# Remainders of chunk 6's sums on VectorE, a semaphore of their own for turned sums, six mask copies ahead of an addition

## The chip, the core and the metric

The kernel runs on one core of a Trainium2 chip. The metric is the device time of one execution in microseconds (us), the median of several runs. PE is TensorE, DVE is VectorE, ACT is ScalarE, POOL is GpSimd, and SP is the engine whose queue issues the DMAs here.

## The reference

Two residual layers over x of shape (2, 1024, 512), in float32:

```python
x = x + gated_delta(layernorm(x), Wq, Wk, Wv, Wo, Wb, bb, Wd, bd)
x = x + ffn(layernorm(x), w1, w2, w3)

# gated_delta: q, k, beta, delta of 64, v of 128; one state S (64 x 128) per batch
S = beta[t][:, None] * S + delta[t][:, None] * outer(k[t], v[t])
o[t] = q[t] @ S                      # then @ Wo

# ffn: weights reduced to -1, 0, 1: clip(round(w / mean|w|))
hidden = sigmoid(x @ Q(w1).T) * (x @ Q(w2).T)     # 512 -> 1408
y = hidden @ Q(w3).T                              # 1408 -> 512
```

## The kernel before

**Tiling.** The 1024 steps are cut into eight chunks (0 to 7) of 128 steps, with both batches side by side. Chunks go through the attention layer one by one. For the second layer two chunks make a group, so there are four groups (g = 0 to 3) of 512 tokens. Group g runs eleven hidden tiles (units u = 0 to 10 of 128 hidden columns), and then four down tiles (m = 0 to 3, one for each chunk and batch), each a sum of 22 matmuls of 512 columns (`down`, L1604). While PE works on group g, the other engines take chunks 2g+2 and 2g+3 through attention, the second normalisation and the split into two 16-bit parts, so that group g+1 can start.

**Fast groups.** Groups 2 and 3 (`FAST`) use a Strassen-like scheme with seven products instead of eight (`product1` to `product7`, each four matmuls of 256 columns, L1622). Products 1, 2 and 4 read the tokens themselves, turned into `xT_N`. Products 3, 5, 6 and 7 read sums and differences of tokens (`xsum`), turned into `xT_S`. Unit u's order on PE is 1, then 5 and 4 of the unit before, 6, 2, then 3 of the unit before, and 7. `product1(g, 0)` is pulled into the last down tile of the group before: it is issued ahead of that tile's last four matmuls. Its result is copied by ACT (`seed`, L936), and `product6(g, 0)`, which follows the down tile, waits for that copy (`seeded`). `product3(g, u)` accumulates into the bank that DVE's `up_b(g, u)` (L1354) must have read.

**Preparing a chunk for a fast group.** DVE `apply` (L1218) writes the normalised tokens, after POOL's six small operations of `norm2` (L523 to L529) have given the scale. The sums are made by DVE (`sums`, L1164 to L1167) for chunks 5 and 7, and by POOL (`sums0`, `sums1`) for chunks 4 and 6. ACT rounds tokens (`xhiN`, L823) and sums (`xhiS`, L828) to 16 bits. The remainders, value minus rounded value, are made by DVE for tokens (`xlo`, L1223). For the sums they are made by DVE for chunks 5 and 7 (`xloS`, one instruction, L1170), and by POOL for chunks 4 and 6 (`xlo`, four instructions, L607). SP then issues two DMA transposes for the chunk (`turn_x`): L434 for tokens, L437 for sums. Both add 16 to `xT_in`, and PE waits once, ahead of `product1(g + 1, 0)`, for the full count of both chunks of the group:

```python
if m == DT - 1 and n == 2 * HT - 4:
    pe.wait_ge(xT_in, 64 * g + 128)
    product1(g + 1, 0)
down(g, m, n, PARTS_IN_TURN)
```

`apply` of chunk 7 waits for `xlo0_ready` of chunk 6, that is for the remainders of chunk 6's sums.

**Order.** Every engine's order is written by hand. Tables such as `DVE_FAST` give for a step the place for chunk 2g+2 and for chunk 2g+3. A negative place u stands for place 15 + u of the group before. `DOWN` (22) is the place in front of the first addition of a fast group (`add_out(g, 0)`, L1309). Steps of one place run in the order of the table. A step at place 14 of a group that isn't fast stands in front of that group's last addition, `add_out(1, 3)`.

**Masks.** For each chunk seven predicated copies (`masks`, L1181) and an eighth (L1189) bring the attention scores of the levels from PSUM into `sc`; PE's `o` step (L1476 to L1485) waits for the eighth. For chunk 6 all stand at place 0 of group 2: behind `add_out(1, 3)`, ahead of `up_b(2, 0)`.

Of the kernel before, what the change touches and what calls it, by code (L numbers as in the profile page):

```python
# [16 lines left out]
def build_gated_delta_ternary_ffn(nc, x, Wq, Wk, Wv, Wo, Wb, bb, Wd, bd, w1, w2, w3, out):  # L17
# [31 lines left out]
    with ctx:  # L49
# [64 lines left out]
        class Scratch:  # L114
            def __init__(self, flat):
# [60 lines left out]
        xhi_ready, xlo0_ready, xlo1_ready, xT_in = (sem("xhi_ready"), sem("xlo0_ready"), sem("xlo1_ready"),  # L176
                                                    sem("xT_in"))
# [77 lines left out]
        def sums_at(which):  # L255
# [21 lines left out]
                    "chainE": (None, 4.5), "masks0": (0, 6.5), "masks1": (0, 7), "masks2": (0, 7.5),  # L277
                    "masks3": (0, 8), "state": (2, None), "resid0": (5, 10.5), "resid1": (5.5, 11),
                    "xlo": (DOWN, DOWN + 1), "xloS": (None, DOWN + 1), "norm2a": (8.5, 11.5), "norm2b": (9, HT + 1),
                    "apply": (10, DOWN), "sums": (None, DOWN)}  # L280
        ACT_FAST = {"gt": (0, None), "oT": (2, 9), "xhiN": (HT, HT + 2), "xhiS": (HT + 1, HT + 2)}
        POOL_FAST = {"fetch": (-1, 0), "sums0": (10, None), "sums1": (11, None), "norm2": (9, HT + 1),
                     "xlo": (HT + 1, None)}
# [65 lines left out]
        def is_fast(c):  # L349

            return c // 2 in FAST

# [40 lines left out]
        def _(sp_):  # L393
# [35 lines left out]
            def turn_x(c):  # L429

                if is_fast(c):
# [6 lines left out]
                                            flat_S[c % 2]).then_inc(xT_in, 16)  # L438
# [53 lines left out]
        def _(pool):  # L492
# [108 lines left out]
            def xlo(c):  # L601
                if c > 1:
                    pool.wait_ge(xT_in, 16 * B * (c - 1))
                if is_fast(c):
                    pool.wait_ge(xhi_ready, B * c + 2)
# [98 lines left out]
        def _(act):  # L704
# [105 lines left out]
            def attn(s, c):  # L810
# [9 lines left out]
                if s == "xhiN":  # L820
                    act.wait_ge(xT_in, 16 * B * (c - 1))
# [4 lines left out]
                if s == "xhiS":  # L826
                    act.wait_ge(sums_ready, c - 2 * FAST[0] + 1)
                    nc.scalar.activation(split_S[c % 2][:, :, 0, :], xsum[:, :, :], ACT.Copy).then_inc(xhi_ready, 1)  # L828
                if s == "xhi":
                    if c > 1:  # L830
                        act.wait_ge(xT_in, 16 * B * (c - 1))
# [177 lines left out]
        def _(dve):  # L1009
# [119 lines left out]
            def attn(s, c):  # L1129
# [31 lines left out]
                if s == "sums":  # L1161
                    dve.wait_ge(xn2_ready, B * c + 2)
                    dve.wait_ge(xhi_ready, B * c)
                    nc.vector.tensor_tensor(xsum[:, 2, :], A11(0), A11(1), ALU.subtract)  # L1164
# [46 lines left out]
                if s == "apply":  # L1211
                    dve.wait_ge(rstd2_ready, c + 1)
                    if c > 0:
                        dve.wait_ge(xhi_ready, B * c)
                        dve.wait_ge(xlo0_ready, c)
# [4 lines left out]
                if s == "xlo" and is_fast(c):  # L1220
                    dve.wait_ge(xT_in, 16 * B * (c - 1))
# [4 lines left out]
                elif s == "xlo":  # L1226
                    if c > 1:
                        dve.wait_ge(xT_in, 16 * B * (c - 1))
# [171 lines left out]
        def _(pe):  # L1400
# [161 lines left out]
            def group(g):  # L1562
                pe.wait_ge(xT_in, 64 * g + 64)
                for u in range(UNITS):
# [15 lines left out]
                    else:  # L1580
                        m = u - HT
                        bank_free(g, 2 * HT + m)
                        for n in range(2 * HT):
# [4 lines left out]
                            if m == DT - 1 and n == 2 * HT - 4 and g + 1 in FAST:  # L1588
                                pe.wait_ge(xT_in, 64 * g + 128)
# [48 lines left out]
            def product6(g, u):  # L1638

                pe.wait_ge(seeded, fast_n(g, u) + 1)  # L1640
# [104 lines left out]
```

## Time and profile before

| | |
|---|---|
| Median of three runs | 322.31 us (322.20 to 322.46) |
| The profiled execution | 321.82 us |
| Its span, first to last instruction | 320.1 us |
| PE, busy | 311.6 us (97%), 2416 matmuls |
| DVE, busy | 226.9 us (71%) |
| ACT, busy | 170.4 us (53%) |
| POOL, busy | 150.0 us (47%) |
| Granted TensorE clock, mean | 0.999 of full speed |

The span is the time on which the steps of one execution can be placed; 1.7 us of the execution's own time lie outside it. Start times below are us from the start of the span. A matmul's end is modelled, so the steps between starts say more on PE than the busy time. A bracket at the end of a timeline row is the idle time of the engine before it and what ended that.

### The profile page before, as it was taken

How to read it: one execution, taken by the hardware profiler on the slowest of the kernel's cores; microseconds unless marked ns; L12 is line 12 of the kernel's file. 1: busy time of each engine (PE TensorE's matmuls, PEld its weight loads, DVE VectorE, ACT ScalarE, POOL GpSimd, SP SyncE). 2: the span in 40 equal slices, each digit the busy share in tenths (PEclk: the TensorE clock that was granted, in tenths of full speed). 3: DMA queues.
4: the chain of work that ended last, by engine and by line, in shares of the span. 5: the costliest groups of instructions: out<-in, count | busy, mean ns of one | idle time of the engine just before them, and what ended most of it. 6: DMA issues, size and time to landing. Idle time of an engine off the chain costs nothing.

```text
span 320.1 us, 6755 instructions
## 1 busy us (share of the span) xinstructions
PE 311.6 (97%) x2416; PEld 200.9 (63%) x2416; DVE 226.9 (71%) x510; ACT 170.4 (53%) x369; POOL 150.0 (47%) x395
## 2 busy tenths in 40 slices
PE   7999999999999999999999999999999999999996
PEld 5888779874545444445445445678976448888545
DVE  6889889899998866277898898559676543454401
ACT  3587896879863772323325215347655216777300
POOL 7298215589932105992016832634468501544300
PEclk9999999999999999999999999999999999999999
DMA  6999900475852441500000807000000691000011
GB/s 177 380 386 394 393 16 0 64 136 104 129 101 49 81 86 45 121 33 2 0 2 0 116 36 180 36 2 0 2 3 0 69 252 45 2 0 2 0 68 66
DMA packets 51953, 28.62 MB, mean 89 GB/s; under 512 B 43728, under 2 KB 44496, under 8 KB 51920
## 3 DMA queue, kind: packets, MB, share of 16 engines
q1 hardware_dynamic: 51600, 28.19, 34.5%
q8 instruction: 19, 0.31, 0.4%
q14 instruction: 14, 0.11, 0.1%
q10 hardware_dynamic: 320, 0.00, 0.0%
HBM read 13.89 MB, written 4.19 MB: 57 GB/s over the span
## 4 chain that ended last, share of the span: by engine, by line
PE 70%; DVE 12%; DMA 5%; issue 4%; SPq 3%; POOL 3%; ACT 3%; DVEq 0%; POOLq 0%; ACTq 0%
PE ffn L1575 17%; PE ffn L1604 15%; PE ffn L1622 14%; PE pd L1622 5%; PE lev L1496 4%; PE ffn L1420 3%; DMA x_sb<-in_L_attn_x_dram 3%; DVE w_nat L1107 2%; DVE X L1120 2%; PE lev L1453 2%; PE pd L1604 2%; SPq L396 2%; PE pd L1430 2%; DVE sc L1181 2%; DMA w_nat<-x_all 1%
## 5 line engine op out<-in xcount | busy, mean ns | idle before, releaser
L1575 PE MATMUL ffn<-w_nat,w12T 128*128 128x512 f16 x352 | 78.1, 379 | 0.5 <-DVE xnT L1320 0.3
L1575 PEld LDWEIGHTS ffn<-w_nat,w12T 128*128 128x128 f16 x352 | 33.7, 98 | 41.6 <-issue 2.1
L1604 PE MATMUL ffn<-w3T,w_nat 128*128 128x512 f16 x264 | 58.0, 379 | 0.0
L1604 PEld LDWEIGHTS ffn<-w3T,w_nat 128*128 128x128 f16 x264 | 25.7, 98 | 31.4 <-ACT w_nat L912 0.7
L1622 PE MATMUL ffn<-w_nat,w12T 128*128 128x256 f16 x312 | 42.1, 273 | 1.2 <-DMA w_nat<-x_all 0.7
L636 POOL TENSOR_TENSOR xnT<-xnT,q 128x256 f32<-128x256 f32 x22 | 16.3, 739 | 51.4 <-ACT xnT L971 39.7
L523 POOL TENSOR_TENSOR ve<-mv,rconst 128x2 f32<-128x2 f32 x12 | 2.6, 218 | 68.7 <-DVE mv L1024 68.7
L1622 PEld LDWEIGHTS ffn<-w_nat,w12T 128*128 128x128 f16 x312 | 30.0, 98 | 6.9 <-DMA w_nat<-x_all 1.2
L1420 PE MATMUL ffn<-xnT,w_proj 128*128 128x256 f32 x128 | 29.5, 384 | 1.2 <-ACT xnT L721 0.8
L906 ACT ACTIVATE xnT<-ffn 128x512 f32<-128x512 f32 x22 | 13.0, 589 | 27.0 <-PE ffn L1575 27.0
L1420 PEld LDWEIGHTS ffn<-xnT,w_proj 128*128 128x128 f32 x128 | 23.7, 190 | 5.1 <-issue 1.0
L1309 DVE SCALAR_TENSOR_TENSOR x_sb<-ffn,x_sb 128x512 f32<-128x512 f32 (+1 forms) x13 | 8.6, 667 | 22.5 <-PE ffn L1604 20.5
L1622 PE MATMUL ffn<-w_nat 128*128 128x256 f16 x144 | 21.6, 273 | 0.1
L1320 DVE SCALAR_TENSOR_TENSOR xnT<-ffn,xnT 128x512 f32<-128x512 f32 x22 | 15.0, 684 | 9.3 <-PE ffn L1575 9.1
L1354 DVE SCALAR_TENSOR_TENSOR q<-ffn,w_nat 128x256 f32<-128x256 f32 x22 | 9.3, 424 | 16.5 <-PE ffn L1622 16.5
L1181 DVE COPY_PREDICATED sc<-mask,lev 128x128 f32<-128x128 uint32 x56 | 18.9, 338 | 2.8 <-PE oc L1467 1.3
L1120 DVE TENSOR_TENSOR X<-X,tmk 128x256 f32<-128x256 f32 x42 | 19.9, 475 | 1.3
L1370 DVE TENSOR_TENSOR w_nat<-xnT,w_nat 128x512 f16<-128x512 f32 x22 | 15.2, 690 | 7.4 <-ACT w_nat L979 7.2
L979 ACT ACTIVATE w_nat<-xnT 128x512 f16<-128x512 f32 x22 | 13.8, 628 | 8.2 <-POOL xnT L644 8.2
L1622 PE MATMUL pd<-w_nat 128*128 128x256 f16 x120 | 18.0, 273 | 0.0
L1325 DVE TENSOR_TENSOR w_nat<-xnT,w_nat 128x512 f16<-128x512 f32 x22 | 16.9, 770 | 0.2
L644 POOL TENSOR_TENSOR xnT<-xnT,q 128x256 f32<-128x256 f32 x22 | 16.6, 753 | 0.6 <-DVE q L1364 0.6
(192 smaller groups left out, 615.6 us busy)
## 6 DMA issues: line engine op xcount, KB each, us to landing
x_sb<-in_L_attn_x_dram SPq DMA_DIRECT2D x16, 256.0 KB, 8.2
out_dram<-x_sb SPq DMA_DIRECT2D x15, 256.0 KB, 2.1
w_nat<-in_L_ffn_w_dram SPq DMA_DIRECT2D x2, 1536.0 KB, 12.3
w_nat<-in_L_ffn_w_dram SPq DMA_DIRECT2D x2, 1408.0 KB, 15.1
w_nat<-in_L_ffn_w_dram SPq DMA_DIRECT2D x2, 1280.0 KB, 12.9
w_proj<-in_L_attn_Wv_dram SPq DMA_DIRECT2D x1, 256.0 KB, 5.5
wo<-in_L_attn_Wo_dram SPq DMA_DIRECT2D x1, 256.0 KB, 14.1
out_dram<-x_sb SPq DMA_DIRECT2D x2, 128.0 KB, 1.7
```

Source lines behind the costliest of these rows:

```text
L636: nc.gpsimd.tensor_tensor(hid32[:, u % 2, HP:2 * HP], sig[:, u % 2, HP:2 * HP], up[:, u % 2, HP:2 * HP], ALU.mult).then_inc(pool_hid, 1)
L644: nc.gpsimd.tensor_tensor(hid32[:, u % 2, 0:HP], sig[:, u % 2, 0:HP], up[:, u % 2, 0:HP], ALU.mult).then_inc(pool_hid, 1)
L979: nc.scalar.activation(hid[:, 0, u, :], hid32[:, u % 2, :], ACT.Copy).then_inc(hi_ready, 1)
L1120: step = nc.vector.tensor_tensor(FG(c, l + 1).rearrange("p (n h) -> p n h", h=h), FG(c, l).rearrange("p (n h) -> p n h", h=h), factors(c, ...
L1181: link(nc.vector.copy_predicated(sc[:, :, :].rearrange("p b (n two h) -> p b n two h", two=2, h=h)[:, :, :, 1, :], level(mask[:, l, :], l) ...
L1320: nc.vector.scalar_tensor_tensor(hid32[:, u % 2, :], bank[(2 * u + 1) % 3][:, :], HS / XS, sig[:, u % 2, :], ALU.mult, ALU.mult).then_inc( ...
L1325: nc.vector.tensor_tensor(hid[:, 1, u - 1, :], hid32[:, (u - 1) % 2, :], hid[:, 0, u - 1, :], ALU.subtract).then_inc(lo_ready, 1)
L1370: nc.vector.tensor_tensor(hid[:, 1, u, :], hid32[:, u % 2, :], hid[:, 0, u, :], ALU.subtract).then_inc(lo_ready, 1)
L1420: done = nc.tensor.matmul(z_bank(c)[:, a * 256:(a + 1) * 256], w[:, t, :], turned(c)[:, t, :, :], start=t == 0, stop=t == DT - 1)
L1575: done = nc.tensor.matmul(bank[n % 3][:, :], w12T[:, a * DT + t, u * P:(u + 1) * P], xT(g)[:, part, t, :], start=t == 0 and part == 0, sto ...
L1604: done = nc.tensor.matmul(down_bank(g, m)[:, :], hid_at(g, part, j, m), w3T[:, j, :], start=n == 0, stop=n == 2 * HT - 1)
L1622: done = nc.tensor.matmul(out[:, 0:HP], weights[:, t, u * P:(u + 1) * P], tokens[:, part, t, :], start=first and t == 0 and part == 0, sto ...
```

## The change

Four things change.

- The remainders of chunk 6's sums move from POOL (four instructions of 256 columns, behind `norm2` of chunk 7) to DVE (one instruction of 1024 columns, behind the remainders of chunk 6's tokens). `apply` of a fast chunk no longer waits for `xlo0_ready`; the sums on DVE do.
- The transposes of sums count on a semaphore of their own, `xS_in`. `product1(g, 0)` waits for the turned tokens alone, and `product6(g, 0)` for the turned sums. ACT's and POOL's waits for the same buffers follow the new counts.
- `product1(g + 1, 0)` stands ahead of the last six matmuls of the down tile, not of the last four.
- The first six mask copies of chunk 6 stand ahead of `add_out(1, 3)`. The seventh and eighth stay behind it.

```diff
-        xhi_ready, xlo0_ready, xlo1_ready, xT_in = (sem("xhi_ready"), sem("xlo0_ready"), sem("xlo1_ready"),
-                                                    sem("xT_in"))
+        xhi_ready, xlo0_ready, xlo1_ready = sem("xhi_ready"), sem("xlo0_ready"), sem("xlo1_ready")
+        xT_in, xS_in = sem("xT_in"), sem("xS_in")
...
-                    "chainE": (None, 4.5), "masks0": (0, 6.5), "masks1": (0, 7), "masks2": (0, 7.5),
+                    "chainE": (None, 4.5), "masks0": (-1, 6.5), "masks1": (-1, 7), "masks2": (-1, 7.5),
                     "masks3": (0, 8), "state": (2, None), "resid0": (5, 10.5), "resid1": (5.5, 11),
-                    "xlo": (DOWN, DOWN + 1), "xloS": (None, DOWN + 1), "norm2a": (8.5, 11.5), "norm2b": (9, HT + 1),
+                    "xlo": (DOWN, DOWN + 1), "xloS": (DOWN, DOWN + 1), "norm2a": (8.5, 11.5), "norm2b": (9, HT + 1),
                     "apply": (10, DOWN), "sums": (None, DOWN)}
         ACT_FAST = {"gt": (0, None), "oT": (2, 9), "xhiN": (HT, HT + 2), "xhiS": (HT + 1, HT + 2)}
-        POOL_FAST = {"fetch": (-1, 0), "sums0": (10, None), "sums1": (11, None), "norm2": (9, HT + 1),
-                     "xlo": (HT + 1, None)}
+        POOL_FAST = {"fetch": (-1, 0), "sums0": (10, None), "sums1": (11, None), "norm2": (9, HT + 1)}
...
+        def tokens_in(c):
+
+            return 16 * sum(1 if is_fast(k) else B for k in range(c + 1))
+
+        def sums_in(c):
+
+            return 16 * len([k for k in range(c + 1) if is_fast(k)])
...
                     sp_.wait_ge(xlo0_ready, c + 1)
                     sp_.dma_start_transpose(xT_S(c // 2)[:, :, :, :, cols].rearrange("p n s t m -> p (n s t) m"),
-                                            flat_S[c % 2]).then_inc(xT_in, 16)
+                                            flat_S[c % 2]).then_inc(xS_in, 16)
...
             def xlo(c):
                 if c > 1:
-                    pool.wait_ge(xT_in, 16 * B * (c - 1))
+                    pool.wait_ge(xT_in, tokens_in(c - 2))
                 if is_fast(c):
+                    if is_fast(c - 2):
+                        pool.wait_ge(xS_in, sums_in(c - 2))
...
                 if s == "xhiN":
-                    act.wait_ge(xT_in, 16 * B * (c - 1))
+                    act.wait_ge(xT_in, tokens_in(c - 2))
...
                 if s == "xhiS":
+                    act.wait_ge(xT_in, tokens_in(c - 2))
+                    if is_fast(c - 2):
+                        act.wait_ge(xS_in, sums_in(c - 2))
                     act.wait_ge(sums_ready, c - 2 * FAST[0] + 1)
...
                 if s == "sums":
                     dve.wait_ge(xn2_ready, B * c + 2)
                     dve.wait_ge(xhi_ready, B * c)
+                    dve.wait_ge(xlo0_ready, c)
...
                     if c > 0:
                         dve.wait_ge(xhi_ready, B * c)
-                        dve.wait_ge(xlo0_ready, c)
+                        if not is_fast(c):
+                            dve.wait_ge(xlo0_ready, c)
                         dve.wait_ge(xlo1_ready, c)
...
             def group(g):
-                pe.wait_ge(xT_in, 64 * g + 64)
+                pe.wait_ge(xT_in, tokens_in(2 * g + 1))
...
-                            if m == DT - 1 and n == 2 * HT - 4 and g + 1 in FAST:
-                                pe.wait_ge(xT_in, 64 * g + 128)
+                            if m == DT - 1 and n == 2 * HT - 6 and g + 1 in FAST:
+                                pe.wait_ge(xT_in, tokens_in(2 * g + 3))
                                 product1(g + 1, 0)
...
             def product6(g, u):
 
                 pe.wait_ge(seeded, fast_n(g, u) + 1)
+                if u == 0:
+                    pe.wait_ge(xS_in, sums_in(2 * g + 1))
                 product(bank_a(u), T2, u, xT_S(g)[:, 1, :, :, :], False).then_inc(m6_done, 1)
...
-                            if m == DT - 1 and n == 2 * HT - 4:
-                                pe.wait_ge(xT_in, 64 * g + 128)
+                            if m == DT - 1 and n == 2 * HT - 6:
+                                pe.wait_ge(xT_in, tokens_in(2 * g + 3))
                                 product1(g + 1, 0)
```

The waits of DVE's `xlo` and of ACT's `xhi` are rewritten with `tokens_in` in the same way; for plain chunks their values stay as they were.

On DVE, at the end of group 1: L1299 is the last of the four weight sums, L1309 is `add_out(1, 3)`, L1181 and L1189 are the masks of chunk 6, L1354 is `up_b(2, 0)`. Before:

```order
L1299 TENSOR_TENSOR w12T<-w12T 128x2816
L1309 SCALAR_TENSOR_TENSOR x_sb<-ffn,x_sb 128x512 [waits down_done,T_ready]
L1181 COPY_PREDICATED sc<-mask,lev 128x128 [waits o_done,levels_done]
L1181 COPY_PREDICATED sc<-mask,lev 128x64x2 [waits dve_steps]
L1181 COPY_PREDICATED sc<-mask,lev 128x32x4 [waits o_done,levels_done,dve_steps]
L1181 COPY_PREDICATED sc<-mask,lev 128x16x8 [waits dve_steps]
L1181 COPY_PREDICATED sc<-mask,lev 128x8x16 [waits o_done,levels_done,dve_steps]
L1181 COPY_PREDICATED sc<-mask,lev 128x4x32 [waits dve_steps]
L1181 COPY_PREDICATED sc<-mask,lev 128x2x64 [waits o_done,levels_done,dve_steps]
L1189 COPY_PREDICATED sc<-ident,oc 128x256 [waits gt_ready,dve_steps]
L1354 SCALAR_TENSOR_TENSOR q<-ffn,w_nat 128x256 [waits u3_ready,m5_done]
```

After (the same lines are L1313, L1323, L1194, L1202 and L1368):

```order
L1313 TENSOR_TENSOR w12T<-w12T 128x2816
L1194 COPY_PREDICATED sc<-mask,lev 128x128 [waits o_done,levels_done,T_ready]
L1194 COPY_PREDICATED sc<-mask,lev 128x64x2 [waits dve_steps]
L1194 COPY_PREDICATED sc<-mask,lev 128x32x4 [waits o_done,levels_done,dve_steps]
L1194 COPY_PREDICATED sc<-mask,lev 128x16x8 [waits dve_steps]
L1194 COPY_PREDICATED sc<-mask,lev 128x8x16 [waits o_done,levels_done,dve_steps]
L1194 COPY_PREDICATED sc<-mask,lev 128x4x32 [waits dve_steps]
L1323 SCALAR_TENSOR_TENSOR x_sb<-ffn,x_sb 128x512 [waits down_done,dve_steps]
L1194 COPY_PREDICATED sc<-mask,lev 128x2x64 [waits o_done,levels_done]
L1202 COPY_PREDICATED sc<-ident,oc 128x256 [waits gt_ready,dve_steps]
L1368 SCALAR_TENSOR_TENSOR q<-ffn,w_nat 128x256 [waits u3_ready,m5_done]
```

The addition moved behind six of the copies; its place before them is now theirs.

On DVE, at the end of group 2's hidden tiles: L1223 makes the remainders of chunk 6's tokens, L1218 is `apply(7)`, L1164 to L1167 are the sums of chunk 7, L1309 is `add_out(2, 0)`. Before:

```order
L1223 TENSOR_TENSOR w_proj<-x_all,w_proj 128x3x256 [waits xhi_ready,xT_in]
L1218 TENSOR_SCALAR x_all<-x_sb,mv,rs 128x512 [waits xlo0_ready,xlo1_ready,xhi_ready,rstd2_ready]
L1218 TENSOR_SCALAR x_all<-x_sb,mv,rs 128x512
L1164 TENSOR_TENSOR x_all<-x_all 128x256 [waits xhi_ready,xn2_ready]
L1165 TENSOR_TENSOR x_all<-x_all 128x256
L1166 TENSOR_TENSOR x_all<-x_all 128x256 [waits dve_steps]
L1167 TENSOR_TENSOR x_all<-x_all 128x256 [waits dve_steps]
L1309 SCALAR_TENSOR_TENSOR x_sb<-pd,x_sb 128x512 [waits down_done]
```

After (L1237, L1183, L1232, L1177 to L1180 and L1323):

```order
L1237 TENSOR_TENSOR w_proj<-x_all,w_proj 128x3x256 [waits xhi_ready,xT_in]
L1183 TENSOR_TENSOR xs<-x_all,xs 128x4x256 [waits xhi_ready]
L1232 TENSOR_SCALAR x_all<-x_sb,mv,rs 128x512 [waits xlo1_ready,xhi_ready,rstd2_ready]
L1232 TENSOR_SCALAR x_all<-x_sb,mv,rs 128x512
L1177 TENSOR_TENSOR x_all<-x_all 128x256 [waits xlo0_ready,xhi_ready,xn2_ready]
L1178 TENSOR_TENSOR x_all<-x_all 128x256
L1179 TENSOR_TENSOR x_all<-x_all 128x256 [waits dve_steps]
L1180 TENSOR_TENSOR x_all<-x_all 128x256 [waits dve_steps]
L1323 SCALAR_TENSOR_TENSOR x_sb<-pd,x_sb 128x512 [waits down_done]
```

The second row, L1183, is new: the remainders of chunk 6's sums. The wait for `xlo0_ready` went from `apply` to the first sum.

On PE, in the last down tile of group 2 (L1604 is `down`, L1622 a product). Before:

```order
L1604 MATMUL pd<-w3T,w_nat 128x512 [waits y_ready]
L1604 MATMUL pd<-w3T,w_nat 128x512 x17
L1622 MATMUL ffn<-w_nat,w12T 128x256 [waits steps_done,sig_b_ready,y_ready,xT_in]
L1622 MATMUL ffn<-w_nat,w12T 128x256 x3
L1604 MATMUL pd<-w3T,w_nat 128x512 x4
L1622 MATMUL ffn<-w_nat 128x256 [waits seeded]
```

After (L1618 and L1636):

```order
L1618 MATMUL pd<-w3T,w_nat 128x512 [waits y_ready]
L1618 MATMUL pd<-w3T,w_nat 128x512 x15
L1636 MATMUL ffn<-w_nat,w12T 128x256 [waits steps_done,sig_b_ready,y_ready,xT_in]
L1636 MATMUL ffn<-w_nat,w12T 128x256 x3
L1618 MATMUL pd<-w3T,w_nat 128x512 x6
L1636 MATMUL ffn<-w_nat 128x256 [waits xS_in,seeded]
```

Two matmuls of the down tile moved behind `product1(3, 0)`, and `product6(3, 0)` has the wait for `xS_in`. The end of group 1 changes in the same way.

## Rows read from the trace of the kernel before

**Rows 1.** What PE waited for in the whole span: total us, times, longest.

```profile
PE ffn L1622 <- DMA w_nat<-x_all: 0.7, 1, 0.7
PE ffn L1622 <- DVE q L1354: 0.4, 1, 0.4
```

**Rows 2.** Timeline of PE, start of group 2: start us, us, instruction, idle before.

```profile
198.22 4.06 PE L1604 MATMUL ffn<-w3T,w_nat 128*128 128x512 f16 x18
202.12 0.60 PE L1622 MATMUL ffn<-w_nat,w12T 128*128 128x256 f16 x4
...
204.94 0.60 PE L1622 MATMUL pd<-w_nat,w12T 128*128 128x256 f16 x4
...
206.69 0.60 PE L1622 MATMUL ffn<-w_nat,w12T 128*128 128x256 f16 x4
207.71 0.61 PE L1622 MATMUL ffn<-w_nat,w12T 128*128 128x256 f16 x4 [0.42 <-DVE q L1354]
```

**Rows 3.** Timeline of PE, start of group 3.

```profile
258.77 4.05 PE L1604 MATMUL pd<-w3T,w_nat 128*128 128x512 f16 x18
263.56 0.61 PE L1622 MATMUL ffn<-w_nat,w12T 128*128 128x256 f16 x4 [0.74 <-DMA w_nat<-x_all]
...
264.87 0.60 PE L1622 MATMUL ffn<-w_nat 128*128 128x256 f16 x4
...
268.13 1.04 PE L1622 MATMUL ffn<-w_nat,w12T 128*128 128x256 f16 x8
269.01 0.60 PE L1622 MATMUL pd<-w_nat 128*128 128x256 f16 x4
```

**Rows 4.** Timeline of DVE, start of group 2.

```profile
198.99 1.58 DVE L1299 TENSOR_TENSOR w12T<-w12T 128x2816 f16<-128x2816 f16 x1
203.69 0.69 DVE L1309 SCALAR_TENSOR_TENSOR x_sb<-ffn,x_sb 128x512 f32<-128x512 f32 x1 [3.12 <-PE ffn L1604]
204.30 2.56 DVE L1181 COPY_PREDICATED sc<-mask,lev 128x128 f32<-128x128 uint32 x7
206.89 0.44 DVE L1189 COPY_PREDICATED sc<-ident,oc 128x256 f32<-128x256 uint32 x1
207.23 0.42 DVE L1354 SCALAR_TENSOR_TENSOR q<-ffn,w_nat 128x256 f32<-128x256 f32 x1
```

**Rows 5.** Timeline of DVE, start of group 3: `up_b(3, 0)`.

```profile
267.46 0.42 DVE L1354 SCALAR_TENSOR_TENSOR q<-ffn,w_nat 128x256 f32<-128x256 f32 x1 [1.70 <-PE ffn L1622]
```

**Rows 6.** Timeline of SP's queue: the issues of chunk 7's two transposes.

```profile
257.38 1.43 SPq L434 DMA_TRANSPOSE w_nat<-w_proj  x1
258.86 2.27 SPq L437 DMA_TRANSPOSE w_nat<-x_all  x1
```

**Rows 7.** DMA issues, 236 to 262 us: count, median us to landing.

```profile
w_nat<-w_proj SPq DMA_TRANSPOSE x2, 3.8
...
w_nat<-x_all SPq DMA_TRANSPOSE x1, 4.6
```

**Rows 8.** Timeline of DVE, end of group 2.

```profile
248.91 0.95 DVE L1223 TENSOR_TENSOR w_proj<-x_all,w_proj 128x768 f16<-128x768 f32 x1
253.17 1.00 DVE L1218 TENSOR_SCALAR x_all<-x_sb,mv,rs 128x512 f32<-128x512 f32 x2 [3.32 <-POOL xs L607]
...
257.27 1.22 DVE L1170 TENSOR_TENSOR x_all<-x_all 128x1024 f16<-128x1024 f32 x1
```

**Rows 9.** Timeline of POOL, end of group 2.

```profile
249.12 0.79 POOL L526 TENSOR_TENSOR rs<-rs,ve 128x2 f32<-128x2 f32 x1
...
250.42 2.55 POOL L607 TENSOR_TENSOR xs<-x_all,xs 128x256 f16<-128x256 f32 x4
```

**Rows 10.** Three stretches: us, then busy time (instructions) of PE, PEld, DVE, ACT, POOL; PEclk, DMA share, GB/s.

```profile
200.67:202.94 2.27, 2.27 (x14) 1.20 (x13) 0.00 (x0) 0.19 (x1) 2.11 (x9) 1.00 0.02 5
204.30:205.20 0.90, 0.86 (x9) 0.64 (x8) 0.87 (x3) 0.58 (x3) 0.90 (x8) 1.00 0.00 0
226.38:227.28 0.90, 0.90 (x11) 0.81 (x9) 0.86 (x3) 0.49 (x3) 0.00 (x0) 1.00 0.00 0
```

More of the change, by code:

```diff
@@ L830, in attn @@
                     if c > 1:
-                        act.wait_ge(xT_in, 16 * B * (c - 1))
+                        act.wait_ge(xT_in, tokens_in(c - 2))
                     if c == 1:
@@ L1220, in attn @@
                 if s == "xlo" and is_fast(c):
-                    dve.wait_ge(xT_in, 16 * B * (c - 1))
+                    dve.wait_ge(xT_in, tokens_in(c - 2))
                     dve.wait_ge(xhi_ready, B * c + 1)
@@ L1227, in attn @@
                     if c > 1:
-                        dve.wait_ge(xT_in, 16 * B * (c - 1))
+                        dve.wait_ge(xT_in, tokens_in(c - 2))
                     dve.wait_ge(xhi_ready, B * c + 2)
```

## The prediction

> **What bounds the kernel now.** I read the page first: PE is busy for 97% of the span, so whatever moves the time must remove a stretch in which PE stands. The second view is the list of what PE waited for. Of its eight entries two lie where the change works [rows 1]: one product waited 0.7 us for turned data, one 0.4 us for DVE's L1354. The third view is PE's timeline at the two places, which shows their full price. Since ends on PE are modelled, I price them by starts.
>
> At the start of group 3, `product1(3, 0)` stands behind 18 down matmuls. At the start of group 2 the same piece ran without a wait: 18 matmuls from 198.22, the product at 202.12, 3.90 us or 0.217 us each [rows 2]. At group 3 they began at 258.77, so the product was due at 262.67 and came at 263.56 [rows 3]. **PE stood 0.89 us.**
>
> At the start of group 2, `product2(2, 1)` starts at 206.69 and `product3(2, 0)` at 207.71 [rows 2]. In group 3 two products in this place, one of them `product3(3, 0)`, take 0.88 us, 268.13 to 269.01 [rows 3], or 0.44 each. So `product3(2, 0)` was due at 207.13. **PE stood 0.58 us**, for `up_b(2, 0)`, which DVE started at 207.23, behind all eight mask copies [rows 4].
>
> **Six masks ahead of the addition.** DVE is free from 200.57 (198.99 plus 1.58) and idle until 203.69, when the down tile is complete and the addition can start [rows 4]. The seven copies and the gap to the eighth take 2.59 us (204.30 to 206.89); without the last, a third of a microsecond by the rest, six take about 2.26. Their inputs are ready: the level matmuls stand ahead of the 18 down matmuls that begin at 198.22 [rows 2]. So they run from 200.7 to 202.9, under the down tile, and leave 0.8 us before the addition, which stays at 203.69. Behind it stand one copy (0.33) and the eighth (0.44): from 204.30 to about 205.1. Then `up_b(2, 0)` waits for its product alone. In group 3, where no masks stand in front, it starts at 267.46, 0.67 ahead of `product2(3, 1)` at 268.13 [rows 3, 5]. The same 0.67 ahead of 206.69 is 206.02; it ends at 206.44, in time for 207.13. The 0.58 us go. The step that is late next is nothing I can find: group 3 runs the same products without that wait at 0.44 each. If the cover under the down tile were gone, the cost would appear at `product1(2, 1)`, which waits for this addition and starts at 204.94 [rows 2]: the addition ends at 204.38, so it has 0.56 to spare, and the copies 0.8 plus 0.56, about 1.4 us in all.
>
> **Remainders of chunk 6's sums on DVE.** DVE ends L1223 at 249.86 and then idles 3.32 us until 253.17, for POOL's four L607, 2.55 us from 250.42 [rows 8, 9]. The same work as one instruction on DVE took 1.22 [rows 8]. It goes into that idle time: 249.8 to 251.1. Then `apply(7)` needs only POOL's `norm2(7)`, which ended by 250.42 [rows 9]. So `apply(7)` could start at 251.1 instead of 253.17, about 2.0 us earlier, and with it the whole chain up to both transposes of chunk 7.
>
> One row speaks against the full 2.0. POOL's tiny L526 took 0.79 us beside DVE's L1223, of which almost all is waiting, since it ended at 249.91 and L1223 at 249.86 [rows 8, 9]. The moved instruction reads two tensors as L1223 does and lies over the small operations that follow, so `norm2(7)` may end only behind it, near 251.3, and `apply(7)` start at 251.5: still 1.7 us earlier. I take 1.7, the side that this row is nearest to; the bounds are 1.7 and 2.1. The Trainium skill's GPSIMD Engine Reference (Key points) says that POOL shares its SBUF interfaces with DVE and contends with DVE instructions that have two SBUF inputs; the trace agrees, with this 0.79 us. By that rule the gain of this move alone is 1.7, without it 2.0; the sum below is the same by both, and the slack differs.
>
> **The semaphore of their own, and product1 two matmuls earlier.** The transposes of chunk 7 were issued at 257.38 (tokens) and 258.86 (sums) [rows 6] and landed 3.8 and 4.6 us later [rows 7]: 261.18 and 263.46. The one wait for both released PE at 263.56. Now `product1(3, 0)`, ahead of six matmuls, is due at 262.67 less 2 x 0.217, at 262.24, and needs only the tokens: 261.18 even without the move, 259.5 with it. `product6(3, 0)` is due one product (0.44) and six matmuls (1.30) later, at 262.24 + 0.44 + 1.30 = 263.98, and needs the sums: 263.46 without the move, 261.8 with it. It came at 264.87 before [rows 3], and 264.87 less 263.98 is the 0.89 again. **Either half of the change removes this wait alone:** the move by 1.7 us against 0.89, the split with 1.06 and 0.52 us of slack. Together the slack is 2.7 and 2.2. The earlier place gives `seed` two matmuls more and removes no matmul: 0 us by itself, between 0 and a loss if the tokens came late. At group 2 all transposes had landed long before.
>
> The added waits cost nothing on the path: on PE `xS_in` is tested behind `seeded`, on ACT `xhiS` waits for a buffer turned a group ago. DVE's seven mask copies, with a wait each, are busy 2.56 of 2.59 us [rows 4], so a met wait is nearly free; bounds 0 and 0.1. SP's queue keeps its order: the transposes move past no other DMA.
>
> **Sum.** 0.58 + 0.89 = 1.47 us, all on PE, and PE then runs in its own pace to the end of the group. The profiled execution had 321.82, so it would be 320.35, with a span of 318.6. The median of the runs is 0.49 above that execution, so I forecast 322.31 - 1.47 = **320.84, say 320.8 us**. Bounds: the small costs give 1.3 to 1.6; single executions scatter by about 0.3 and more, so 320.4 to 321.3 for this case.
>
> **The rivals.**
> - *Only group 3 gains.* Something behind `product3(2, 0)`, the ACT copy for `product7(2, 1)` or the `o` step, waits in its turn and takes the 0.58 back. For: at group 2 an `o` step follows that group 3 does not have. Against: it waited for the eighth mask, which now is 2.2 us earlier. 322.31 - 0.89 = 321.4.
> - *Only group 2 gains.* The transposes land later than 3.8 and 4.6 us after their issue, beside a store and chunk 6's transposes, which now all start earlier. They would have to be 2.2 us later. 322.31 - 0.58 = 321.7.
> - *Nothing.* The prices by starts are wrong, or both stalls come back a few products later: 322.3.
> - *Slower: POOL holds the masks.* Their new place lies beside POOL's work for chunk 7; POOL is busy 2.11 of 2.27 us there [rows 10] and was still busy at 205.20. If no copy could run while POOL works, the 2.26 us would begin behind 205.2 and end near 207.5, the addition near 208.2, and `product1(2, 1)` would start at 208.3 instead of 204.94: 3.36 lost, 1.47 gained, 324.2. It decides from the point where the copies end 1.4 us late, and makes the kernel slower from 2.9 us late (1.4 + 1.47). Against: the first two copies took 0.87 in 0.90 us with POOL busy throughout, and 0.86 with POOL idle [rows 10]. POOL does not hold them. The GPSIMD Engine Reference (Key points) of the Trainium skill names instructions with two SBUF inputs; these copies read one input from SBUF and one from PSUM, and the trace agrees with this case too.
>
> **How the numbers follow.** A measurement of this kernel can tell about 0.2%, 0.64 us, from no change. Forecast 0.79; only group 3 gains 0.06; a gain of more than 1.9 0.02: these are faster by over 0.2%, 0.87. Only group 2 gains 0.05 and nothing 0.04: within it, 0.09. Slower 0.04, for the rival above and for what I do not see. The range 320.3 to 321.6 takes in the forecast with its bounds and the case in which only group 3 gains; it leaves out the other rivals (0.13) and the ends of the forecast.
>
> **What would show it.** In the profile of the changed kernel: DVE's six copies start about 200.7 and the addition still about 203.7; no idle before `product3(2, 0)`, which starts 0.44 behind `product2(2, 1)`; the `o` step 0.58 earlier. At the end of group 2, measured from PE's starts: `apply(7)` follows the new L1183 within 0.5 us and is released by POOL's `norm2`, not by remainders; `product1(3, 0)` starts 16 x 0.217 = 3.47 us behind the tile's first matmul, and `product6(3, 0)` 1.74 behind it. PE's list of waits loses both rows. I am wrong if `product1(2, 1)` waits for the addition, if `product1` or `product6` of group 3 waits for a transpose, or if group 2 takes longer between its first product and its last by what its start gained.

## The result, and the profile after

| | before | after |
|---|---|---|
| Median of five runs each, same chip | 322.31 us | 320.75 us |
| Lowest and highest | 321.77 to 322.69 | 320.41 to 321.29 |
| The profiled execution | 321.82 us | 321.29 us |
| Its span | 320.1 us | 319.6 us |
| PE, busy in the span | 311.6 us | 311.4 us |

The ratio of the runs is 0.9953, with a 95% interval of 0.9939 to 0.9966: 1.5 us or about 0.5% faster. The forecast was 320.8 us.

The two profiled executions differ by only 0.5 us. The changed one lost 0.9 us in its first ten microseconds, before anything that the change touches: PE's first transposes of tokens stood 0.80 us for DVE's normalised tokens of chunk 0, which is not so before.

The changed kernel, timeline of PE, start of the kernel (us from the start, duration, instruction, idle before and what ended it):

```profile
1.66 4.88 PE L1521 MATMUL lev<-ident 128*128 128x256 f16 x24 [1.66 <-POOL ident L510]
7.34 0.66 PE L1422 MATMUL ffn<-ident,x_all 128*128 128x128 f32 x4 [0.80 <-DVE x_all L1068]
```

Before:

```profile
6.46 0.66 PE L1408 MATMUL ffn<-ident,x_all 128*128 128x128 f32 x4
```

At the start of group 2 the changed trace is 0.98 us behind (199.20 against 198.22 [rows 2]). So absolute times of the two traces can't be set side by side, and this text compares distances from a matmul of the same stage.

The changed kernel, timeline of PE, start of group 2:

```profile
199.20 3.63 PE L1618 MATMUL ffn<-w3T,w_nat 128*128 128x512 f16 x16
202.67 0.60 PE L1636 MATMUL ffn<-w_nat,w12T 128*128 128x256 f16 x4
203.10 1.46 PE L1618 MATMUL ffn<-w3T,w_nat 128*128 128x512 f16 x6
204.40 0.60 PE L1636 MATMUL ffn<-w_nat 128*128 128x256 f16 x4
204.83 0.60 PE L1636 MATMUL ffn<-w_nat,w12T 128*128 128x256 f16 x4
205.47 0.61 PE L1636 MATMUL ffn<-w_nat 128*128 128x256 f16 x4
205.92 0.60 PE L1636 MATMUL pd<-w_nat,w12T 128*128 128x256 f16 x4
...
207.67 1.04 PE L1636 MATMUL ffn<-w_nat,w12T 128*128 128x256 f16 x8
208.54 0.60 PE L1636 MATMUL pd<-w_nat 128*128 128x256 f16 x4
```

The row of 207.67 is `product2(2, 1)` and, with no step in between, `product3(2, 0)`; `product7` follows at 208.54, 0.87 us for two products. Before, the second of them came 1.02 behind the first, with an idle time in front [rows 2]. That idle time is gone, and PE's list of waits has neither of the two rows any more.

The changed kernel, timeline of PE, start of group 3:

```profile
259.16 3.62 PE L1618 MATMUL pd<-w3T,w_nat 128*128 128x512 f16 x16
262.61 0.60 PE L1636 MATMUL ffn<-w_nat,w12T 128*128 128x256 f16 x4
263.05 1.46 PE L1618 MATMUL pd<-w3T,w_nat 128*128 128x512 f16 x6
264.34 0.60 PE L1636 MATMUL ffn<-w_nat 128*128 128x256 f16 x4
```

`product1(3, 0)` starts 3.45 us behind the first of the down matmuls, `product6(3, 0)` 5.18; before it was 6.10 [rows 3]. From the first of the down matmuls at group 2 to the first at group 3 the distance is 259.16 - 199.20 = 59.96 us; before it was 258.77 - 198.22 = 60.55 [rows 2, 3]. So 0.59 us went at the start of group 2 and 0.92 at the start of group 3. From `product6(3, 0)` to the end of the span it is 55.2 us in both traces: nothing was given back.

The changed kernel, timeline of DVE, start of group 2:

```profile
199.97 1.58 DVE L1313 TENSOR_TENSOR w12T<-w12T 128x2816 f16<-128x2816 f16 x1
201.59 2.26 DVE L1194 COPY_PREDICATED sc<-mask,lev 128x128 f32<-128x128 uint32 x6
204.67 0.69 DVE L1323 SCALAR_TENSOR_TENSOR x_sb<-ffn,x_sb 128x512 f32<-128x512 f32 x1 [0.82 <-PE ffn L1618]
205.28 0.29 DVE L1194 COPY_PREDICATED sc<-mask,lev 128x128 f32<-128x128 uint32 x1
205.60 0.45 DVE L1202 COPY_PREDICATED sc<-ident,oc 128x256 f32<-128x256 uint32 x1
207.00 0.42 DVE L1368 SCALAR_TENSOR_TENSOR q<-ffn,w_nat 128x256 f32<-128x256 f32 x1 [0.95 <-PE ffn L1636]
```

Six copies took 2.26 us and left 0.82 before the addition. `up_b(2, 0)` (L1368) now waits for its product and starts 0.67 us ahead of `product2(2, 1)`, as group 3's does [rows 5]. The stretch of the six copies, in the view of busy times (us, then PE, PEld, DVE, ACT, POOL, clock, DMA share, GB/s), shows POOL beside them nearly all the time, and the clock at its full level of 2.4 GHz:

```profile
201.59:203.85 2.26, 2.26 (x14) 1.26 (x13) 2.08 (x6) 0.55 (x2) 2.10 (x8) 1.00 0.02 5
```

The changed kernel, timeline of DVE, end of group 2:

```profile
249.30 0.95 DVE L1237 TENSOR_TENSOR w_proj<-x_all,w_proj 128x768 f16<-128x768 f32 x1
250.16 1.22 DVE L1183 TENSOR_TENSOR xs<-x_all,xs 128x1024 f16<-128x1024 f32 x1
251.75 1.00 DVE L1232 TENSOR_SCALAR x_all<-x_sb,mv,rs 128x512 f32<-128x512 f32 x2 [0.37 <-POOL rs L536]
```

and of POOL beside it:

```profile
249.51 0.79 POOL L533 TENSOR_TENSOR rs<-rs,ve 128x2 f32<-128x2 f32 x1
250.39 1.05 POOL L534 TENSOR_SCALAR rs<-rs 128x2 f32<-128x2 f32 x1
251.52 0.20 POOL L536 TENSOR_TENSOR rs<-rs 128x2 f32<-128x2 f32 x1
```

`apply(7)` (L1232) starts 2.45 us behind L1237 instead of 4.26 [rows 8], and `norm2` releases it. POOL's L534 on two columns took 1.05 us: it ends at 251.44, just behind the moved instruction at 251.38.

### The profile page after: what moved, and what is told of

The parts are those of the page before. It is cut to its first block, busy times and chain, and to the rows that moved or that the text cites. A ratio compares the mean times of both kernels' runs of the same rounds, so it can differ in the third digit from the quotient of the medians.

```text
span 319.6 us, 6752 instructions
## 1 busy us (share of the span) xinstructions
PE 311.4 (97%) x2416; PEld 201.0 (63%) x2416; DVE 227.4 (71%) x511; ACT 170.5 (53%) x369; POOL 149.0 (47%) x391
## 4 chain that ended last, share of the span: by engine, by line
PE 77%; DVE 10%; DMA 4%; SPq 3%; ACT 2%; issue 2%; DVEq 0%; ACTq 0%
PE ffn L1618 18%; PE ffn L1589 17%; PE ffn L1636 16%; PE pd L1636 5%; PE pd L1618 5%; PE lev L1510 4%; DMA x_sb<-in_L_attn_x_dram 4%; PE ffn L1434 3%; DVE w_nat L1119 2%; DVE X L1132 2%; PE lev L1467 2%; SPq L403 2%; PE pd L1444 2%; PE oc L1494 1%; DVE abs_part L1099 1%
## 5 line engine op out<-in xcount | busy, mean ns | idle before, releaser
L1618 PE MATMUL ffn<-w3T,w_nat 128*128 128x512 f16 x264 | 58.0, 379 | 0.0
L1618 PEld LDWEIGHTS ffn<-w3T,w_nat 128*128 128x128 f16 x264 | 25.7, 98 | 31.4 <-ACT w_nat L924 0.7
L1636 PE MATMUL ffn<-w_nat,w12T 128*128 128x256 f16 x312 | 41.9, 273 | 0.0
L1636 PEld LDWEIGHTS ffn<-w_nat,w12T 128*128 128x128 f16 x312 | 30.2, 98 | 5.2 <-issue 0.7
L1323 DVE SCALAR_TENSOR_TENSOR x_sb<-ffn,x_sb 128x512 f32<-128x512 f32 (+1 forms) x13 | 8.7, 669 | 22.1 <-PE ffn L1618 20.1
L1368 DVE SCALAR_TENSOR_TENSOR q<-ffn,w_nat 128x256 f32<-128x256 f32 x22 | 9.3, 425 | 17.4 <-PE ffn L1636 17.4
L1636 PE MATMUL ffn<-w_nat 128*128 128x256 f16 x144 | 21.6, 273 | 0.1
L1194 DVE COPY_PREDICATED sc<-mask,lev 128x128 f32<-128x128 uint32 x56 | 19.0, 339 | 2.8 <-PE oc L1481 1.2
L1384 DVE TENSOR_TENSOR w_nat<-xnT,w_nat 128x512 f16<-128x512 f32 x22 | 15.2, 690 | 7.4 <-ACT w_nat L991 7.2
L1636 PE MATMUL pd<-w_nat 128*128 128x256 f16 x120 | 18.0, 273 | 0.0
L1339 DVE TENSOR_TENSOR w_nat<-xnT,w_nat 128x512 f16<-128x512 f32 x22 | 16.1, 733 | 0.2
```

What stands on the lines that cost most here:

```text
L1194: link(nc.vector.copy_predicated(sc[:, :, :].rearrange("p b (n two h) -> p b n two h", two=2, h=h)[:, :, :, 1, :], level(mask[:, l, :], l) ...
L1339: nc.vector.tensor_tensor(hid[:, 1, u - 1, :], hid32[:, (u - 1) % 2, :], hid[:, 0, u - 1, :], ALU.subtract).then_inc(lo_ready, 1)
L1384: nc.vector.tensor_tensor(hid[:, 1, u, :], hid32[:, u % 2, :], hid[:, 0, u, :], ALU.subtract).then_inc(lo_ready, 1)
L1618: done = nc.tensor.matmul(down_bank(g, m)[:, :], hid_at(g, part, j, m), w3T[:, j, :], start=n == 0, stop=n == 2 * HT - 1)
L1636: done = nc.tensor.matmul(out[:, 0:HP], weights[:, t, u * P:(u + 1) * P], tokens[:, part, t, :], start=first and t == 0 and part == 0, sto ...
```

## The experiments

Each kernel was timed in five rounds beside the kernel before on the same chip. "Ratio" is to that kernel, with its 95% interval; it is computed from the single runs, so it can differ by up to 0.0007 from the quotient of the two medians. Two distances come from each trace, both between starts on PE: at group 2 from the first down matmul behind the level matmuls to `product1(2, 2)` (the first product behind the `o` step), at group 3 from the first matmul of the last down tile to `product6(3, 0)`.

| kernel | median us (before) | ratio | at group 2 | at group 3 |
|---|---|---|---|---|
| before | 322.31 | | 11.65 | 6.10 |
| the change | 320.75 (322.31) | 0.9953 (0.9939 to 0.9966) | 11.06 | 5.18 |
| masks alone | 321.51 (322.20) | 0.9978 (0.9969 to 0.9988) | 11.06 | 6.12 |
| split and early product1 | 321.15 (322.20) | 0.9968 (0.9955 to 0.998) | 11.65 | 5.19 |
| split alone | 321.00 (322.26) | 0.9958 (0.994 to 0.9976) | 11.65 | 5.19 |
| move alone | 321.26 (322.20) | 0.9966 (0.9952 to 0.9979) | 11.65 | 5.18 |
| early product1 alone | 322.53 (322.20) | 1.0007 (0.9991 to 1.0023) | 11.64 | 6.54 |
| change without the move | 320.79 (322.08) | 0.9953 (0.9941 to 0.9965) | 11.06 | 5.19 |
| masks and move, no split | 320.69 (322.08) | 0.9953 (0.9941 to 0.9965) | 11.06 | 5.19 |
| six masks twice | 321.50 (322.26) | 0.9978 (0.9962 to 0.9995) | 12.03 | 5.19 |
| all eight masks ahead | 320.55 (322.26) | 0.9944 (0.9925 to 0.9963) | 11.06 | 5.19 |
| product6 early too | 320.51 (322.26) | 0.9942 (0.9925 to 0.996) | 11.00 | (below) |

The intervals are 0.2 to 0.4% wide: the times tell 0.6 us from nothing, but hardly 0.9 from 0.6. The distances, which repeat within 0.02 us, tell the parts apart.

### Masks alone

Against the kernel before:

```diff
-                    "chainE": (None, 4.5), "masks0": (0, 6.5), "masks1": (0, 7), "masks2": (0, 7.5),
+                    "chainE": (None, 4.5), "masks0": (-1, 6.5), "masks1": (-1, 7), "masks2": (-1, 7.5),
```

> The kernel before with the masks' new place alone. Theory (two stalls that add up): product3(2,0) starts 0.44 us behind product2(2,1) instead of 1.02, everything behind it 0.58 us earlier, group 3 keeps its wait of 0.89 us for the transposes, so product6(3,0) still starts 6.10 us behind the first of the 18 down matmuls ahead of it. Time 0.58 us (0.2%) under before. Rival (the two halves lean on each other): the shorter group 2 brings the transposes of chunk 7 no earlier, its gain is lost in a longer wait at group 3, and the time stays as before.

Measured: 0.7 us under before, 0.59 of it at group 2; the distance at group 3 stayed at 6.12. The first theory stands. The wait at group 3 did not grow, since the transposes moved with PE's progress through group 2: the tokens' transpose of chunk 7 was issued 1.39 us ahead of the down tile's first matmul in both traces (256.80 against 258.19, and 257.38 against 258.77 [rows 3, 6]). PE:

```profile
258.19 4.05 PE L1604 MATMUL pd<-w3T,w_nat 128*128 128x512 f16 x18
263.00 0.61 PE L1622 MATMUL ffn<-w_nat,w12T 128*128 128x256 f16 x4 [0.77 <-DMA w_nat<-x_all]
```

### Split with the earlier product1, and split alone

Against the kernel before, in both kernels, with the waits of ACT and POOL as in the change:

```diff
-                                            flat_S[c % 2]).then_inc(xT_in, 16)
+                                            flat_S[c % 2]).then_inc(xS_in, 16)
...
-                                pe.wait_ge(xT_in, 64 * g + 128)
+                                pe.wait_ge(xT_in, tokens_in(2 * g + 3))
...
+                if u == 0:
+                    pe.wait_ge(xS_in, sums_in(2 * g + 1))
```

and in the first kernel alone:

```diff
-                            if m == DT - 1 and n == 2 * HT - 4:
+                            if m == DT - 1 and n == 2 * HT - 6:
```

> The kernel before with the semaphore of their own for turned sums and product1 two matmuls earlier, POOL still making chunk 6's remainders and the masks in their old place. Theory: the tokens are there 1.0 us before product1(3,0), the sums 0.5 us before product6(3,0); product6(3,0) starts 5.2 us behind the first of the down matmuls instead of 6.10; time 0.89 us under before (0.28%). Rival (the transposes are simply late, and only the remainders on VectorE bring them early enough): product6(3,0) waits for the sums, and the gain is under 0.4 us.

> The kernel before with the semaphore of their own for turned sums alone; product1 ahead of the last four matmuls as before, remainders on POOL, masks in their old place. Theory: the same as with product1 two matmuls earlier, product6(3,0) 5.2 us behind the first of the down matmuls, time 0.89 us under before; the earlier place of product1 is worth 0. Rival: with only four matmuls between, ScalarE's copy of product1 comes late for product6(3,0) once the wait is gone, and 0.1 to 0.3 us of the gain are missing against the run with product1 earlier.

Measured: 5.19 us at group 3 in both, 1.1 and 1.3 us under before. The split alone, the issue of the last transpose, its time to landing in the DMA view, and `product6(3, 0)`:

```profile
258.97 2.39 SPq L445 DMA_TRANSPOSE w_nat<-x_all  x1
w_nat<-x_all SPq DMA_TRANSPOSE x1, 4.7
264.06 0.60 PE L1635 MATMUL ffn<-w_nat 128*128 128x256 f16 x4
```

It landed at 263.67, 0.39 ahead of the product that needs it. The predicted slack was 0.52. The semaphore of its own is enough, and the two matmuls' earlier place is worth nothing: ACT's copy of `product1` was in time with four matmuls as well.

### Move alone

Against the kernel before:

```diff
-                    "xlo": (DOWN, DOWN + 1), "xloS": (None, DOWN + 1), "norm2a": (8.5, 11.5), "norm2b": (9, HT + 1),
+                    "xlo": (DOWN, DOWN + 1), "xloS": (DOWN, DOWN + 1), "norm2a": (8.5, 11.5), "norm2b": (9, HT + 1),
...
-        POOL_FAST = {"fetch": (-1, 0), "sums0": (10, None), "sums1": (11, None), "norm2": (9, HT + 1),
-                     "xlo": (HT + 1, None)}
+        POOL_FAST = {"fetch": (-1, 0), "sums0": (10, None), "sums1": (11, None), "norm2": (9, HT + 1)}
```

> The kernel before with chunk 6's remainders on VectorE alone, one semaphore for all transposes and product1 in its old place. Theory: apply(7) starts 1.7 us earlier (2.1 if POOL were not held up by the moved instruction), the last transpose lands 1.7 us earlier, product1(3,0) starts 3.90 us behind the first of the 18 down matmuls with no wait; time 0.89 us under before. Rival: VectorE's and GpSimd's mutual hold eats the gain, apply(7) starts under 0.9 us earlier, and part of the wait at product1(3,0) stays.

Measured: 5.18 us at group 3, 0.9 us under before. `apply(7)` starts 2.45 us behind the remainders of chunk 6's tokens instead of 4.26, so 1.8 us earlier, between the 1.7 expected and the bound of 2.1. The move is enough too.

### Early product1 alone

Against the kernel before, at both groups, with one semaphore:

```diff
-                            if m == DT - 1 and n == 2 * HT - 4:
+                            if m == DT - 1 and n == 2 * HT - 6:
                                 pe.wait_ge(xT_in, 64 * g + 128)
```

> The kernel before with product1 two matmuls earlier alone, one semaphore for all transposes, remainders on POOL. Theory: product1(3,0) is due 0.44 us earlier and still starts when the last transpose has landed; six instead of four matmuls then stand between it and product6(3,0), which starts 6.5 us behind the first of the down matmuls instead of 6.10. Time 0.43 us above before. Rival (the earlier copy of product1's result is what helps): product6(3,0) starts earlier than before, and the time falls.

Measured: 6.54 us at group 3, 0.44 longer, and a ratio whose interval includes 1. The timeline of PE has the whole of it:

```profile
258.73 3.62 PE L1604 MATMUL pd<-w3T,w_nat 128*128 128x512 f16 x16
263.53 0.61 PE L1622 MATMUL ffn<-w_nat,w12T 128*128 128x256 f16 x4 [1.18 <-DMA w_nat<-x_all]
263.98 1.46 PE L1604 MATMUL pd<-w3T,w_nat 128*128 128x512 f16 x6
265.27 0.60 PE L1622 MATMUL ffn<-w_nat 128*128 128x256 f16 x4
```

`product1` waits until the same moment, two matmuls that could have covered the wait now stand behind it, and PE idles 0.44 us more (1.18 against 0.74 [rows 3]). In the distance this part is a loss without one of the other two; the times can't show so little.

### Both halves of group 3's part, each taken out of the change

The first is the changed kernel with the move undone, `apply`'s wait for `xlo0_ready` included:

```diff
-                    "xlo": (DOWN, DOWN + 1), "xloS": (DOWN, DOWN + 1), "norm2a": (8.5, 11.5), "norm2b": (9, HT + 1),
+                    "xlo": (DOWN, DOWN + 1), "xloS": (None, DOWN + 1), "norm2a": (8.5, 11.5), "norm2b": (9, HT + 1),
...
-        POOL_FAST = {"fetch": (-1, 0), "sums0": (10, None), "sums1": (11, None), "norm2": (9, HT + 1)}
+        POOL_FAST = {"fetch": (-1, 0), "sums0": (10, None), "sums1": (11, None), "norm2": (9, HT + 1),
+                     "xlo": (HT + 1, None)}
...
-                    dve.wait_ge(xlo0_ready, c)
...
-                        if not is_fast(c):
-                            dve.wait_ge(xlo0_ready, c)
+                        dve.wait_ge(xlo0_ready, c)
```

The second is the kernel before with the two edits of tables, of *masks alone* and of *move alone*, together.

> The changed kernel with chunk 6's remainders back on POOL; masks, semaphore and product1's place as changed. Theory (either half removes the wait at group 3): product6(3,0) 5.2 us behind the first down matmul of its tile, as in the changed kernel, though the last transpose lands 1.6 us later against that matmul; time as the changed kernel, 1.5 us under before. Rival (with group 2 shorter by 0.58 us the transposes come too late without the move): product6(3,0) waits for the sums, and the gain is 1.2 us or less.

> The kernel before with the masks' new place and the remainders on VectorE; one semaphore for all transposes and product1 ahead of four matmuls, as before. Theory: the last transpose lands 0.9 us before product1(3,0) is due, so nothing waits there; time as the changed kernel, 1.5 us under before. Rival: product1(3,0) waits for a transpose, gain 1.2 us or less.

Measured: 11.06 and 5.19 us in both, and both ratios equal the change's own (by the medians 1.3 and 1.4 us under before, too near to the rivals' 1.2 to decide; the distances do). In the first the last transpose was issued at 258.88 and took 4.7 us in the DMA view, so it landed 0.39 us ahead of `product6(3, 0)` at 263.97. In the second it was issued at 256.92 and landed near 261.6, 0.9 ahead of `product1(3, 0)` at 262.53.

### Six masks twice

Against the changed kernel, behind the loop over the levels in the mask step; the copies write the same values again:

```diff
+                    if c == 6 and s == "masks2":
+                        for l in (0, 1, 2, 3, 4, 5):
+                            n, h = P // 2 ** (l + 1), 2 ** l
+                            link(nc.vector.copy_predicated(
...
```

> The changed kernel with the six mask copies ahead of the addition issued twice (the result is the same). Theory: twelve copies take 4.5 us from 1.6 us behind the last weight sum's start, so they end 1.5 us behind the end of the down tile instead of 0.8 ahead of it; product1(2,1) waits for the addition, about 0.9 to 1.1 us; the time is that much above the changed kernel, still 0.4 to 0.6 under before. It measures the slack of the masks, which the prediction gave as 1.4 us. Rival (a copy is held by POOL's work beside it, and the second six, still beside POOL, take longer): over 5 us for the twelve, product1(2,1) 1.5 us or more late, and the time at or above before.

Measured: 0.97 us longer at group 2 than the change, and a median 0.8 us under before. DVE:

```profile
201.06 2.25 DVE L1194 COPY_PREDICATED sc<-mask,lev 128x128 f32<-128x128 uint32 x6
203.35 2.23 DVE L1201 COPY_PREDICATED sc<-mask,lev 128x128 f32<-128x128 uint32 x6
205.62 0.69 DVE L1330 SCALAR_TENSOR_TENSOR x_sb<-ffn,x_sb 128x512 f32<-128x512 f32 x1
```

and PE:

```profile
206.37 0.61 PE L1643 MATMUL pd<-w_nat,w12T 128*128 128x256 f16 x4 [0.81 <-DVE x_sb L1330]
```

The second six cost 2.29 us from start to start. Only 0.97 of it reached PE, so the slack behind the six copies is 2.29 - 0.97 = 1.3 us, where the prediction had 1.4: PE's product starts 0.06 behind the end of the addition (205.62 + 0.69), which the prediction left out. POOL was busy for all of the 2.23 us of the second six and for 2.09 of the 2.25 of the first, and neither took longer than the other by more than 0.02. The rival that POOL holds them falls.

### All eight masks ahead

Against the changed kernel:

```diff
-                    "masks3": (0, 8), "state": (2, None), "resid0": (5, 10.5), "resid1": (5.5, 11),
+                    "masks3": (-1, 8), "state": (2, None), "resid0": (5, 10.5), "resid1": (5.5, 11),
```

> The changed kernel with all eight mask copies ahead of the addition. Theory: the last two add 0.75 us, the copies end about where the down tile ends (0.8 us of room), the addition starts up to 0.1 us later, which its 0.56 us of slack at product1(2,1) hides; time as the changed kernel, within 0.1 us. Rival: the eighth copy waits for ScalarE's gate copy, which stands behind product1(2,0)'s result copy, and this wait passes on to the addition and to product1(2,1): over 0.2 us slower than the changed kernel.

Measured: the distances of the change, 11.06 and 5.19. DVE's addition starts 5.40 us behind the first down matmul (203.50 against 198.10) instead of 5.47 (204.67 against 199.20): 0.07 earlier, where up to 0.1 later was expected. The copies end at 203.55, so no room is left ahead of the addition. The first theory stands; the seventh and eighth copies could go ahead as well, and it gains nothing more.

### product6 early too

In the change `product7(g, 0)` starts 0.64 us behind `product2(g, 0)` (205.47 against 204.83), where a product needs 0.44.

Against the changed kernel, at both groups:

```diff
+                            if m == DT - 1 and n == 2 * HT - 2 and g + 1 in FAST:
+                                pe.wait_ge(T_ready, 4)
+                                product6(g + 1, 0)
                             down(g, m, n, PARTS_IN_TURN)
...
-                    product6(g, k)
+                    if k > 0:
+                        product6(g, k)
```

> The changed kernel with product6 of unit 0 (groups 2 and 3) pulled into the down tile as well, ahead of its last two matmuls. In the changed kernel product7(g,0) starts 0.64 us behind product2(g,0) instead of 0.44, since ScalarE's copy of product6's result ends just before it. Theory: with two down matmuls more in between this 0.20 us goes at both groups, time 0.4 us (0.12%) under the changed kernel. Rival: product6 then waits for ScalarE's copy of product1, only four matmuls ahead of it, or the next product waits instead, and the time stays.

Measured: at group 2 11.00 us instead of 11.06. At group 3, to `product7(3, 1)`, 267.71 - 258.51 = 9.20 us instead of 268.49 - 259.16 = 9.33. That makes 0.19 us of the 0.40 expected. PE at group 2:

```profile
204.24 0.60 PE L1639 MATMUL ffn<-w_nat,w12T 128*128 128x256 f16 x4
204.68 0.60 PE L1639 MATMUL ffn<-w_nat 128*128 128x256 f16 x4
205.26 0.61 PE L1639 MATMUL pd<-w_nat,w12T 128*128 128x256 f16 x4
```

the row of its weight loads at the same place, and DVE's addition:

```profile
205.25 0.33 PEld L1639 LDWEIGHTS pd<-w_nat,w12T 128*128 128x128 f16 x4 [0.26 <-DVE x_sb L1323]
```

```profile
204.51 0.69 DVE L1323 SCALAR_TENSOR_TENSOR x_sb<-ffn,x_sb 128x512 f32<-128x512 f32 x1 [1.26 <-PE ffn L1621]
```

`product7(2, 0)` now follows `product2(2, 0)` in 0.44, and the 0.20 us are gone there. But `product6` was also the cover of the last addition: with two products instead of three between the end of the down tile and `product1(2, 1)`, that one stands for the addition, which ends at 205.20. At group 3 it is the same addition again: it ends at 265.03, and the product starts at 265.08. The rival, that the next product waits instead, took half of the gain. The expectation had left out the 0.56 us of slack that the prediction itself had named at this product: the cover shrank by a product and the 0.20 us, 0.64 in all. The median, 320.51 us, can't be told from the change's.

## Why the prediction was right

**The prices by starts.** 0.58 at group 2 and 0.89 at group 3 were predicted; 0.59 and 0.92 came, 1.51 in the traces. The medians moved by 1.56 us. Priced by idle times in the list of waits [rows 1], 0.4 and 0.7, the sum would have been 1.1.

**The masks.** Predicted: six copies in 2.26 us, 0.8 of room, the addition unmoved, `up_b(2, 0)` 0.67 ahead of `product2(2, 1)`. All came so (2.26, 0.82, 0.67). The addition starts 5.47 us behind the first down matmul both times. Masks alone bring their share, and doubled they show the slack, 1.3 us for 1.4.

**The move.** Predicted: `apply(7)` 1.7 us earlier rather than 2.1, since the moved instruction would hold up POOL's `norm2`. It came 1.8 earlier. The row that I leant on, 0.79 us for L526 [rows 9], was read rightly as waiting: the same line took 0.19 to 0.20 in its other eleven executions before. And it came again: POOL's L534, which took 0.19 with no DVE instruction beside it (L535 in the trace of the split alone), took 1.05 under the moved one. The Trainium skill's GPSIMD Engine Reference (Key points), on contention with DVE instructions of two SBUF inputs, agrees with this row.

**The split, and that either half is enough.** Predicted: slack of 2.7 and 2.2 us with both. The changed trace has the tokens issued at 255.96 and the sums at 257.62, landing after 3.9 and 4.5 us, so 2.75 us ahead of `product1(3, 0)` and 2.2 ahead of `product6(3, 0)`. Each half alone brings 5.2 us at group 3, in both directions: added to before, and taken from the change. This was the part with the widest claim, and the five kernels with only one of the halves bear it out. Without the move the slack was thin, 0.39 us against one transpose's 4.7. The earlier `product1` was put at 0 by itself, or a loss if its data came late: 0 with the split, 0.44 lost alone.

**The rivals.** *Only group 3* and *only group 2* fall with the distances: no stall came back. *Nothing* falls with the distances and the ratio. *POOL holds the masks* falls with the doubled copies.

**What was off.** I expected a span of 318.6 us in the profile; it had 319.6. This execution was 0.98 us behind the one before at the start of group 2, 0.88 of it already at PE's first transposes of tokens (7.34 against 6.46), which no step of mine covers. In between the difference wasn't steady, so that the wait at the start is the whole of it is not shown. The median came within 0.1 us of the forecast, 320.75 against 320.84. Among runs that lie 0.9 us apart so close a hit is luck in part; the evidence for the mechanism is the distances.

## What to carry to other kernels

- Price a wait by the distance between starts, against the same piece of the program where it does not wait. The idle times in the list of waits understated both, by 0.15 us and 0.16 us.
- Two fixes of one wait did not add up: run each alone. Here a semaphore that counts only what the consumer reads did the same as taking 1.8 us out of the producer's chain; and issuing the consumer earlier without either only moved its cover behind it, for a loss of 0.44 us.
- Work that several engines wait for (an addition that frees a bank) can give its place to other work as far as its consumer has slack, and that slack is spent once: the masks had 1.3 us of it, the addition alone 0.56, and pulling a product out of the cover took 0.64.

## What the hardware showed that I had not expected

The transpose of chunk 6's sums did not land clearly earlier when it was issued earlier. Distances here are from the start of DVE's remainders of chunk 6's tokens (L1223 before). With the remainders on POOL (six traces) the transpose was issued 4.1 us behind that start and took 4.5 to 5.3 us to landing, so it landed 8.6 to 9.4 behind. With the move (six traces) it was issued 2.3 behind and took 6.4 to 6.6, so it landed 8.7 to 8.9 behind. In the move-alone trace:

```profile
w_nat<-w_proj SPq DMA_TRANSPOSE x2, 3.9
w_nat<-xs SPq DMA_TRANSPOSE x1, 6.5
```

So the 1.8 us were gone in the queue, while the transposes of chunk 7 kept their 3.8 to 4.0 and 4.4 to 4.7. Nobody waits for that landing here.

The store and chunk 7's first transpose, which come next in the queue, are not the cause: they are issued 3.5 and 4.4 us behind it both before and after. What changed is the distance to the transpose of tokens just ahead of it, 1.3 us with the move and 3.1 without. The transpose of chunk 4's sums shows the same pattern without any move. Before:

```profile
177.43 1.44 SPq L434 DMA_TRANSPOSE w_nat<-w_proj  x1
178.91 2.38 SPq L437 DMA_TRANSPOSE w_nat<-xs  x1
```

It was issued 1.48 us behind its tokens' and took 6.6, with 9.9 us to SP's next DMA. Over all twelve traces these transposes from `xs` took 6.4 to 6.8 us when issued 1.3 to 1.5 behind their tokens', 5.2 to 6.2 at 2.2, and 4.5 to 5.3 at 3.1. But the sums of chunks 5 and 7, which lie in `x_all`, took 4.4 to 4.7 at 1.5 to 1.7 behind theirs. Why the one buffer is slower close behind another transpose and the other isn't was not tried, and stays open.
